# A windowed-attention stage with its exponentials two units ahead, its softmax division on VectorE, and its PSUM banks shared out anew

## The chip, the cores and the metric

The kernel runs on one core of a Trainium2 chip. The metric is device time in microseconds (us) for one launch; lower is better. The profile names the engines PE (TensorE; PEld is its weight load), ACT (ScalarE), DVE (VectorE), POOL (GpSimd) and SP (SyncE, which here issues DMAs).

## The reference

The program is two transformer blocks over `x` of shape (8, 512, 128), f32: windowed attention, a mixture of experts, dense attention, and an FP4 feed-forward layer. The change touches the first attention only. For each of the 8 sequences:

```python
h = layernorm(x) * (1 + ca) + sa
xn = rms_norm(h)
q, k, v = split(xn @ w_qkv.T)            # 16 heads of 64
q, k = rope(q), rope(k)
attn = softmax(where(0 <= q_pos - k_pos <= 32, q @ k.T / 8, -1e9))
x = x + ga * ((attn @ v) @ w_out.T)      # per head, then the output projection
```

## The kernel before, in words

`phase_attention0` writes each engine's program out by hand, in a block per engine. The engines meet only at semaphores, and each takes its own instructions in order. A sequence is cut into four **quads** of four heads, and a quad into four **units** (`t` = 0 to 3) of 128 queries, so a sequence has `UNITS` = 16 units; unit 16 of a sequence is unit 0 of the next. `turns` runs `body(b, last)` once for the first sequence, in a loop for the middle six and once more for the last.

A unit `u` goes through these steps:

- PE `score` (L438, L446) makes masked scores for four heads in `psS`, two banks for each parity of `u`, two units ahead of the unit whose turn it is.
- DVE `maxes` (L621) takes the row maxima of the whole unit, also two ahead.
- ACT `exps` (L549) makes the exponentials with their sums: four instructions of 96 columns, each followed by a read of its accumulator. It is called in halves of two heads, `j` = 0 and 1, one unit ahead.
- DVE `inverse` (L653) inverts two sums, and POOL `divide` (L732) multiplies the two heads' `prob` by them, per half.
- PE transposes `prob` into `psT` (L504), ACT copies it to `probT` (L601), PE multiplies by `v` into `psO` (L524), and ACT `copy_oT` (L583) copies the product one unit later.

Beside the units, the projections of the quad after next are made in six **pieces** (`PIECES`), placed by `PLAN`. In each quad four pieces are halves of q and k (L459) and two are v (L464), which `VALUE` numbers. All go through one bank, `psQ`, which ACT `piece` copies out (L560, L565). A q or k piece then has three followers: SP `swap` (L765) sends four DMAs that exchange rotary halves, POOL `cosines` (L722) multiplies the piece by the cosine table, and, two units later, DVE `sines` (L627) multiplies the swapped copy by the sine table and `rope` (L636) adds the two. DVE runs `sines` and `rope` in the midst of its other work for the unit. `windows` (L770 to L772) copies v with DMAs into the layout that L524 reads.

At the end of a sequence `out_project` (L480, 64 instructions) goes through `psQ` too, after a wait for all pieces. DVE then multiplies and adds the result to `x` (L710, L712) and measures it (L365) before it goes on to the next unit's work. `turn_x` (L474), after unit 7's product, brings in the next sequence's input and also waits for all pieces made so far.

This is what ACT does in one unit, and what PE does around the product:

```python
exps(b, u + 1, 0)                        # ACT
wait(act, turned, b * UNITS + u + 1)
nc.scalar.copy(probT[:, :, :], psT[0:KW, :, :]).then_inc(probT_ready, 1)
exps(b, u + 1, 1)
copy_oT(b, u - 1)
for q, m in pieces_at(g, t, last):
    piece(b, q, m)
```

Of the kernel before, what the change touches and what calls it, by code (L numbers as in the profile page):

```python
# [367 lines left out]
def phase_attention0(nc, k):  # L368
# [5 lines left out]
    with ExitStack() as ctx:  # L374
# [15 lines left out]
        psO = ctx.enter_context(nc.psum_tensor("psO", [P, 2, 512], F32))  # L390
        psQ = ctx.enter_context(nc.psum_tensor("psQ", [P, 512], F32))
# [16 lines left out]
        VALUE = (2, 5)  # L408
        PLAN = ((0,), (1, 2), (3,), (4, 5))

        def half_of(m):
            return m - m // 3
# [17 lines left out]
        def _(pe):  # L430
# [21 lines left out]
            def project(b, q, m):  # L452

                wait(pe, piece_out, b * QUADS * PIECES + q * PIECES + m)
                g = q % QUADS
                if m not in VALUE:
                    half = half_of(m)
                    col = (half % 2) * H0 * D + (2 * g + half // 2) * P
                    last = nc.tensor.matmul(psQ[:, :], k.wqkvT[:, col:col + P], xnT[:, :], start=True, stop=True)  # L459
                else:  # L460
                    col = 2 * H0 * D + g * 4 * D
                    for i in range(2):
                        t = 2 * VALUE.index(m) + i
                        last = nc.tensor.matmul(psQ[:, i * 4 * D:(i + 1) * 4 * D], xnT[:, t * P:(t + 1) * P],  # L464
                                                k.wqkvT[:, col:col + 4 * D], start=(i == 0), stop=True, skip_group_check=True)
                last.then_inc(projected, 1)

            def turn_x(b, pieces):
# [4 lines left out]
                for t in range(TILES):  # L473
                    last = nc.tensor.transpose(psQ[:, t * P:(t + 1) * P], xn[:, t, :], k.ident)  # L474
                last.then_inc(x_turned, 1)

            def out_project(b, pairs, first, last_):
                for t in range(TILES):
                    for p in pairs:
                        last = nc.tensor.matmul(psQ[:, t * C:(t + 1) * C], oT[:, p, t * P:(t + 1) * P], k.woT[:, p, :],  # L480
# [14 lines left out]
            def body(b, last):  # L495
                for u in range(UNITS):
# [16 lines left out]
                    for q, m in pieces[:1]:  # L513
# [3 lines left out]
                    wait(pe, oT_ready, b * UNITS + u - 1)  # L517
                    if t == 0:
                        wait(pe, v_placed, (b * QUADS + g + 1) * 48)
                    for i in range(2):  # L520
                        for a in range(2):
                            for j in range(2):
                                hd = slice((2 * i + j) * D, (2 * i + j + 1) * D)
                                ins = nc.tensor.matmul(psO[D * j:D * j + D, u % 2, i * P + a * HALF:i * P + (a + 1) * HALF],  # L524
# [3 lines left out]
                    for q, m in pieces[1:]:  # L528
                        project(b, q, m)
# [13 lines left out]
        def _(act):  # L543
            def exps(b, u, j):
                s = u % 2
                if j == 0:
                    wait(act, max_ready, b * UNITS + u + 1)
                for i in range(2):
                    last = nc.scalar.activation(prob[:, s, 2 * j + i, :], psS[:, s, j, i * KW:(i + 1) * KW], ACT.Exp,  # L549
                                                bias=nmax[:, s, 2 * j + i:2 * j + i + 1],  # L550
# [1430 lines left out]
```

## Time and profile before

| | |
|---|---|
| time, median of 3 runs | 1468.14 us (1468.02 to 1470.77) |
| the profiled execution's own time | 1453.94 us |
| its span | 1452.1 us |
| mean granted TensorE clock | 0.852 |
| busy over the whole span | PE 1064.6, DVE 787.6, POOL 660.8, ACT 615.4 us |
| the stage that changes | about 34 to 700 us of the span |

The profiled execution is 14.2 us below the median of the runs. The units of the changed stage begin near 78 us, after a start in which twelve pieces are projected one after another, and end near 690 us. Its sequences are told apart by L710, which DVE executes once in each.

### The profile page before, as it was taken

To read this page: it belongs to the slowest core of one execution; us is meant where nothing else is said; L and a number is where in the kernel's file an instruction comes from. 1 tells how busy PE (TensorE), PEld (TensorE's weight loads), DVE (VectorE), ACT (ScalarE), POOL (GpSimd) and SP (SyncE) were. 2 spreads that over 40 slices of the span, in tenths; PEclk is the share of its full clock that TensorE was granted. 3 is DMA by queue.
4 is the path that set the end of the run, shared out by engine and by line. 5 is a ranking of instruction groups with operands and counts; after the bars stand their busy time and mean duration, and the time that the engine had idled before them with its cause. 6 is when DMAs were issued, how large, how long until landed. Compare 5 with 4: busy or idle time off the path is not lost. (4 is left out here: it accounts for less than half of the span.)

```text
span 1452.1 us, 26107 instructions
## 1 busy us (share of the span) xinstructions
PE 1064.6 (73%) x8506; PEld 698.1 (48%) x8506; DVE 787.6 (54%) x1755; ACT 615.4 (42%) x2039; POOL 660.8 (46%) x575
## 2 busy tenths in 40 slices
PE   2688888888889888888612596675299999636665
PEld 1245555555556555556502264344056666424444
DVE  4265555656564656543656441112236665488985
ACT  1257464757575666655101231221045555323222
POOL 1366474757575766653100678786200000145451
PEclk9579899999999999999555798888569999868777
DMA  9234243433334342431401144344200000000000
GB/s 258 68 87 110 63 103 88 103 92 99 97 82 112 79 119 73 108 85 37 118 2 55 36 74 69 61 90 78 67 1 1 1 0 0 1 0 7 15 14 22
DMA packets 85374, 93.57 MB, mean 64 GB/s; under 512 B 18752, under 2 KB 58032, under 8 KB 85312
## 3 DMA queue, kind: packets, MB, share of 16 engines
q1 hardware_dynamic: 73184, 81.50, 21.5%
q0 software_dynamic: 11840, 10.76, 5.1%
q8 instruction: 34, 0.56, 0.2%
q10 hardware_dynamic: 288, 0.53, 0.1%
q14 instruction: 28, 0.23, 0.1%
HBM read 24.36 MB, written 10.70 MB: 24 GB/s over the span
## 5 line engine op out<-in xcount | busy, mean ns | idle before, releaser
L732 POOL TENSOR_TENSOR prob<-prob,prob_rsum 128x192 f32<-128x192 f32 x256 | 202.4, 791 | 219.8 <-DVE prob_rsum L653 219.8
L722 POOL TENSOR_TENSOR qk_cos<-qk_raw,const 128x512 f32<-128x512 f32 x128 | 179.4, 1402 | 31.2 <-ACT qk_raw L560 30.5
L549 ACT ACTIVATE prob<-psS,neg_max 128x96 f32<-128x96 f32 x512 | 171.5, 347 | 18.6 <-DVE neg_max L621 18.6
L459 PE MATMUL psQ<-a_xnT,weights 128*128 128x512 f32 x256 | 161.0, 714 | 8.6 <-ACT v_tok L565 4.4
L627 DVE TENSOR_TENSOR qk_swapped<-qk_swapped,const 128x512 f32<-128x512 f32 x128 | 105.1, 821 | 104.7 <-DMA qk_swapped<-qk_raw 103.7
L504 PE MATMUL psT<-const,prob 128*96 128x128 f32 x512 | 95.5, 288 | 59.2 <-POOL prob L732 58.9
L636 DVE TENSOR_TENSOR qk_roped<-qk_cos,qk_swapped 128x512 f32<-128x512 f32 x128 | 124.5, 973 | 2.1
L1308 POOL DMA_INDIRECT ex_rows<-rows,ex_index x64 | 66.4, 1038 | 127.1 <-DMA ex_index<-lists 107.9
L524 PEld LDWEIGHTS psO<-probT,v_windows 96*64 96x64 f32 x2048 | 73.6, 143 | 103.2 <-issue 67.2
L1318 POOL DMA_INDIRECT sums<-ex_y,ex_index x64 | 103.1, 1611 | 29.6 <-issue 18.6
L549 ACT ACTIVATION_READ_ACCUMULATOR prob<-psS,neg_max 128x1 f32 x512 | 107.2, 209 | 0.0
L601 ACT COPY probT<-psT 96x512 f32<-96x512 f32 x128 | 74.3, 580 | 74.8 <-PE psT L504 73.1
L560 ACT COPY qk_raw<-psQ 128x512 f32<-128x512 f32 x128 | 76.4, 597 | 49.8 <-PE psQ L459 44.8
L504 PEld LDWEIGHTS psT<-const,prob 128*96 128x96 f32 x512 | 51.8, 127 | 89.2 <-POOL prob L732 73.7
L1254 ACT ACTIVATE ex_hidden<-ex_psH,ex_b 128x512 f32<-128x512 f32 x64 | 43.5, 687 | 117.2 <-PE ex_psH L1214 61.9
L524 PE MATMUL psO<-probT,v_windows 96*64 96x64 f32 x2048 | 91.6, 235 | 2.1 <-ACT probT L601 2.0
L1214 PE MATMUL ex_psH<-ex_hT,ex_w 128*128 128x512 f32 x128 | 72.8, 714 | 26.0 <-ACT ex_hidden L1254 25.2
L464 PE MATMUL psQ<-weights,a_xnT 128*128 128x256 f32 x256 | 78.3, 432 | 10.5 <-ACT qk_raw L560 5.1
L326 POOL TENSOR_TENSOR rstd<-a_veps,neghalf 128x4 f32<-128x4 f32 (+1 forms) x8 | 8.5, 1057 | 167.9 <-DVE a_veps L320 167.9
L1518 PEld LDWEIGHTS a_psO<-a_v,a_probT 128*128 128x128 f32 x512 | 65.8, 198 | 36.9 <-ACT a_probT L1566 27.6
L621 DVE TENSOR_REDUCE neg_max<-psS 128x4 f32<-128x384 f32 x128 | 70.3, 549 | 23.2 <-PE psS L446 23.2
L653 DVE RECIPROCAL prob_rsum<-prob_sum 128x2 f32<-128x2 f32 x256 | 40.2, 157 | 74.9 <-ACT prob L549 74.7
(282 smaller groups left out, 2120.4 us busy)
## 6 DMA issues: line engine op xcount, KB each, us to landing
qk_swapped<-qk_raw SPq DMA_DIRECT2D x512, 64.0 KB, 2.0
v_windows<-v_tok SPq DMA_DIRECT2D x32, 384.0 KB, 4.4
v_windows<-v_tok SPq DMA_DIRECT2D x32, 256.0 KB, 3.6
mod<-mod_rows SPq DMA_DIRECT2D x8, 512.0 KB, 7.7
ex_w<-in_L_ffn_W SPq DMA_DIRECT2D x16, 256.0 KB, 3.1
v_windows<-v_tok SPq DMA_DIRECT2D x32, 96.0 KB, 2.1
x<-in_L_attn_x POOLq DMA_DIRECT2D x4, 512.0 KB, 12.6
rows<-rt_h SPq DMA_DIRECT2D x8, 256.0 KB, 2.4
```

Of the source, the lines that this page charges most:

```text
L459: last = nc.tensor.matmul(psQ[:, :], k.wqkvT[:, col:col + P], xnT[:, :], start=True, stop=True)
L464: last = nc.tensor.matmul(psQ[:, i * 4 * D:(i + 1) * 4 * D], xnT[:, t * P:(t + 1) * P], k.wqkvT[:, col:col + 4 * D], start=(i == 0), stop= ...
L504: ins = nc.tensor.transpose(psT[0:KW, i, :], prob[:, u % 2, i, :], k.ident)
L524: ins = nc.tensor.matmul(psO[D * j:D * j + D, u % 2, i * P + a * HALF:i * P + (a + 1) * HALF], vw[:, par, a, t, hd], probT[:, 2 * j + i, a ...
L549: last = nc.scalar.activation(prob[:, s, 2 * j + i, :], psS[:, s, j, i * KW:(i + 1) * KW], ACT.Exp, bias=nmax[:, s, 2 * j + i:2 * j + i + ...
L560: ins = nc.scalar.copy(raw[:, half, :], psQ[:, :])
L601: nc.scalar.copy(probT[:, :, :], psT[0:KW, :, :]).then_inc(probT_ready, 1)
L627: nc.vector.tensor_tensor(swp[:, half, :], swp[:, half, :], k.const[:, K_SIN:K_SIN + T], ALU.mult).then_inc(sin_done, 1)
L636: nc.vector.tensor_tensor(qk[:, q % 2, half // 2, half % 2, :], rcos[:, half, :], swp[:, half, :], ALU.add).then_inc(roped, 1)
L722: nc.gpsimd.tensor_tensor(rcos[:, half, :], raw[:, half, :], k.const[:, K_COS:K_COS + T], ALU.mult).then_inc(cos_done, 1)
L732: nc.gpsimd.tensor_tensor(heads, heads, rsum[:, u % 2, 2 * j:2 * j + 2].unsqueeze(2).to_broadcast([P, 2, KW]), ALU.mult).then_inc(normed_r ...
L1318: nc.gpsimd.indirect_dma_start(k.sums, bass.IndirectOffsetOnAxis(ap=index2[:, par, n:n + 1], axis=0), y[:, par, n, :], None, compute_op=AL ...
```

## The change

The code does five things.

- **Exponentials.** `exps` is no longer called in halves. ACT's unit is now: copy `probT`, copy `oT`, all four exponentials of unit `u + 2`, then the pieces.
- **Division.** POOL's `divide` is gone. DVE's `divide` inverts all four sums in one instruction, waits for it, and multiplies all four heads in one instruction of 384 columns. It opens DVE's unit, for unit `u + 1`; `sines`, `maxes` of `u + 2` and `rope` follow.
- **Banks.** `psO` shrinks from two banks to 256 columns of one, and `psQ` grows from one bank to two, used in turn by the parity of the piece. PE's wait before a piece is for the piece before the last one.
- **Plan.** v pieces are now numbers 3 and 5 instead of 2 and 5, and both pieces of a unit with two come before the product.
- **Waits.** The product of unit `u` waits for the copy of unit `u - 1`'s product, where it waited for that of unit `u - 2`.

```diff
-        psO = ctx.enter_context(nc.psum_tensor("psO", [P, 2, 512], F32))
-        psQ = ctx.enter_context(nc.psum_tensor("psQ", [P, 512], F32))
+        psO = ctx.enter_context(nc.psum_tensor("psO", [P, 2 * P], F32))
+        psQ = ctx.enter_context(nc.psum_tensor("psQ", [P, 2, 512], F32))
...
-        VALUE = (2, 5)
-        PLAN = ((0,), (1, 2), (3,), (4, 5))
+        VALUE = (3, 5)
+        PLAN = ((0,), (1,), (2, 3), (4, 5))
...
-                wait(pe, piece_out, b * QUADS * PIECES + q * PIECES + m)
+                wait(pe, piece_out, b * QUADS * PIECES + q * PIECES + m - 1)
...
-                    last = nc.tensor.matmul(psQ[:, :], k.wqkvT[:, col:col + P], xnT[:, :], start=True, stop=True)
+                    last = nc.tensor.matmul(psQ[:, m % 2, :], k.wqkvT[:, col:col + P], xnT[:, :], start=True, stop=True)
...
-                        if i % 2 == 0:
-                            wait(pe, normed_ready, b * 2 * UNITS + 2 * u + i // 2 + 1)
+                        if i == 0:
+                            wait(pe, normed_ready, b * UNITS + u + 1)
...
-                    for q, m in pieces[:1]:
+                    for q, m in pieces:
                         project(b, q, m)
 
                     wait(pe, probT_ready, b * UNITS + u + 1)
-                    wait(pe, oT_ready, b * UNITS + u - 1)
+                    wait(pe, oT_ready, b * UNITS + u)
...
                     ins.then_inc(applied, 1)
-                    for q, m in pieces[1:]:
-                        project(b, q, m)
...
-                    more = not (last and u + 1 >= UNITS)
-                    if more:
-                        exps(b, u + 1, 0)
                     wait(act, turned, b * UNITS + u + 1)
                     nc.scalar.copy(probT[:, :, :], psT[0:KW, :, :]).then_inc(probT_ready, 1)
-                    if more:
-                        exps(b, u + 1, 1)
                     if u > 0:
                         copy_oT(b, u - 1)
+                    if not (last and u + 2 >= UNITS):
+                        exps(b, u + 2)
                     for q, m in pieces_at(g, t, last):
                         piece(b, q, m)
...
-            def inverse(b, u, j):
-
-                wait(dve, exp_done, b * 2 * UNITS + 2 * u + j + 1)
-                nc.vector.reciprocal(rsum[:, u % 2, 2 * j:2 * j + 2], psum_[:, u % 2, 2 * j:2 * j + 2]).then_inc(rsum_ready, 1)
+            def divide(b, u):
+
+                n = b * UNITS + u + 1
+                wait(dve, exp_done, n)
+                nc.vector.reciprocal(rsum[:, u % 2, :], psum_[:, u % 2, :]).then_inc(rsum_ready, 1)
+                wait(dve, rsum_ready, n)
+                nc.vector.tensor_tensor(prob[:, u % 2, :, :], prob[:, u % 2, :, :],
+                                        rsum[:, u % 2, :].unsqueeze(2).to_broadcast([P, 4, KW]), ALU.mult).then_inc(normed_ready, 1)
...
+                    if more:
+                        divide(b, u + 1)
                     if roping:
                         sines(b, q, half)
-                    if more:
-                        inverse(b, u + 1, 0)
+                    if not (last and u + 2 >= UNITS):
+                        maxes(b, u + 2)
                     if roping:
                         rope(b, q, half)
-                    if not (last and u + 2 >= UNITS):
-                        maxes(b, u + 2)
-                    if more:
-                        inverse(b, u + 1, 1)
...
-                    if not (last and u + 1 >= UNITS):
-                        divide(b, u + 1, 0)
-                        divide(b, u + 1, 1)
```

On DVE, one unit in the third quad of a sequence stood like this before (L653 inverts sums, L627 is `sines`, L636 `rope`, L621 `maxes`):

```order
L627 TENSOR_TENSOR qk_swapped<-qk_swapped,const 128x512 [waits swapped2]
L653 RECIPROCAL prob_rsum<-prob_sum 128x2 [waits exp_done]
L636 TENSOR_TENSOR qk_roped<-qk_cos,qk_swapped 128x512 [waits scored,cos_done,sin_done]
L621 TENSOR_REDUCE neg_max<-psS 128x4 [waits scored]
L653 RECIPROCAL prob_rsum<-prob_sum 128x2 [waits exp_done]
```

A unit in the changed kernel (L649 and L651 are the division, L622 `sines`, L616 `maxes`, L631 `rope`):

```order
L649 RECIPROCAL prob_rsum<-prob_sum 128x4 [waits exp_done]
L651 TENSOR_TENSOR prob<-prob,prob_rsum 128x384 [waits rsum_ready]
L622 TENSOR_TENSOR qk_swapped<-qk_swapped,const 128x512 [waits swapped1]
L616 TENSOR_REDUCE neg_max<-psS 128x4 [waits scored]
L631 TENSOR_TENSOR qk_roped<-qk_cos,qk_swapped 128x512 [waits scored,cos_done,sin_done]
```

`maxes` has moved from behind `rope` to ahead of it, and it now stands behind both the wait for the exponentials and the multiplication of 384 columns.

On ACT, a unit with two pieces before, from its first exponential on (L601 copies `probT`, L583 `oT`, L560 and L565 the pieces):

```order
L549 ACTIVATE prob,prob_sum<-psS,neg_max 128x96 [waits max_ready]
L549 ACTIVATE prob,prob_sum<-psS,neg_max 128x96
L601 COPY probT<-psT 96x512 [waits turned]
L549 ACTIVATE prob,prob_sum<-psS,neg_max 128x96 x2
L583 COPY oT<-psO 128x2x128 [waits applied]
L560 COPY qk_raw<-psQ 128x512 [waits roped,projected]
L565 COPY v_tok<-psQ 128x512 [waits projected]
```

The same in the changed kernel (L547 exponentials, L596 `probT`, L581 `oT`, L558 and L563 pieces):

```order
L596 COPY probT<-psT 96x512 [waits turned]
L581 COPY oT<-psO 128x2x128 [waits applied]
L547 ACTIVATE prob,prob_sum<-psS,neg_max 128x96 [waits max_ready]
L547 ACTIVATE prob,prob_sum<-psS,neg_max 128x96 x3
L558 COPY qk_raw<-psQ 128x512 [waits roped,projected]
L563 COPY v_tok<-psQ 128x512 [waits projected]
```

The exponentials are now those of two units ahead, and both piece copies stand right behind the last of them.

## Rows read from the trace of the kernel before

**Rows 1.** Busy time by windows, third sequence: window, PE, PEld, DVE, ACT, POOL, clock, DMA.
```profile
241.00:318.00 77.00, 67.32 (x743) 43.24 (x742) 46.10 (x97) 48.39 (x193) 48.80 (x49) 0.96 0.37 94
```
**Rows 2.** Instructions of line L710, once per sequence: durations in ns, first and last start.
```profile
L710 DVE TENSOR_TENSOR y_mul<-psQ,mod x8: 690/692/693, 162.8 to 687.9; 128x512 f32<-128x512 f32 x8
L710 DVEq FUSED_REGOPS  x6: 82/82/82, 241.1 to 622.5; - x6
```
**Rows 3.** Waits from 85 to 690 us: us in total, times, longest.
```profile
DVE qk_swapped L627 <- DMA qk_swapped<-qk_raw: 88.6, 56, 3.9
...
PE psT L504 <- POOL prob L732: 57.1, 98, 2.1
```
**Rows 4.** Timeline of PE in unstalled units: start, duration, line, what it writes and reads.
```profile
278.28 0.60 PE L504 MATMUL psT<-const,prob 128*96 128x128 f32 x4
...
281.14 0.42 PE L504 MATMUL psT<-const,prob 128*96 128x128 f32 x2
...
285.07 1.13 PE L464 MATMUL psQ<-weights,a_xnT 128*128 128x256 f32 x4
```
**Rows 5.** Timeline of ACT and DVE: exponentials, their followers, and a maximum.
```profile
78.58 0.34 ACT L549 ACTIVATE prob<-psS,neg_max 128x96 f32<-128x96 f32 x1 [1.18 <-DVE neg_max L621]
...
79.76 0.22 ACT L549 ACTIVATION_READ_ACCUMULATOR prob<-psS,neg_max 128x1 f32 x1
...
266.13 0.22 ACT L549 ACTIVATION_READ_ACCUMULATOR prob<-psS,neg_max 128x1 f32 x1
266.38 0.17 DVE L653 RECIPROCAL prob_rsum<-prob_sum 128x2 f32<-128x2 f32 x1 [1.56 <-ACT prob L549]
...
322.33 0.55 DVE L621 TENSOR_REDUCE neg_max<-psS 128x4 f32<-128x384 f32 x1
...
322.92 0.34 ACT L549 ACTIVATE prob<-psS,neg_max 128x96 f32<-128x96 f32 x1 [2.08 <-DVE neg_max L621]
```
**Rows 6.** Timeline of DVE at a sequence's end.
```profile
318.17 0.69 DVE L710 TENSOR_TENSOR y_mul<-psQ,mod 128x512 f32<-128x512 f32 x1 [9.56 <-PE psQ L480]
...
319.01 0.69 DVE L712 TENSOR_TENSOR x<-x,y_mul 128x512 f32 x1 [0.16 <-DVE y_mul L710]
...
320.91 0.69 DVE L627 TENSOR_TENSOR qk_swapped<-qk_swapped,const 128x512 f32<-128x512 f32 x1 [0.18 <-issue]
```
**Rows 7.** Groups of DVE, 241.1 to 318.2 us: count, busy us, mean ns, idle before.
```profile
L347 DVE TENSOR_SCALAR a_h<-x,mean,rstd 128x128 f32 x4 | 1.3, 381 | 0.0
```
**Rows 8.** Timeline of DVE where its instructions meet one of POOL.
```profile
81.81 1.76 DVE L627 TENSOR_TENSOR qk_swapped<-qk_swapped,const 128x512 f32<-128x512 f32 x1
...
83.60 1.64 DVE L636 TENSOR_TENSOR qk_roped<-qk_cos,qk_swapped 128x512 f32<-128x512 f32 x1
```
**Rows 9.** Timeline of POOL over the same stretch.
```profile
82.98 1.71 POOL L722 TENSOR_TENSOR qk_cos<-qk_raw,const 128x512 f32<-128x512 f32 x1
```
**Rows 10.** Timeline: a piece copied by ACT, and the cosine product that follows on POOL.
```profile
300.25 0.58 ACT L560 COPY qk_raw<-psQ 128x512 f32<-128x512 f32 x1 [0.30 <-PE psQ L459]
...
300.92 1.26 POOL L722 TENSOR_TENSOR qk_cos<-qk_raw,const 128x512 f32<-128x512 f32 x1
```
**Rows 11.** Timeline of PE: the output projection.
```profile
310.58 7.41 PE L480 MATMUL psQ<-weights,oT 128*128 128x128 f32 x64 [0.68 <-ACT v_tok L565]
```
**Rows 12.** Timeline of PE at its longest stall of a sequence.
```profile
245.94 0.49 PE L504 MATMUL psT<-const,prob 128*96 128x128 f32 x2 [2.12 <-POOL prob L732]
```
**Rows 13.** Busy time by windows behind that stall, columns as in rows 1.
```profile
246.00:253.00 7.00, 6.36 (x43) 3.64 (x44) 5.03 (x11) 2.83 (x11) 4.80 (x5) 0.51 0.11 28
```
**Rows 14.** Timeline of PE projecting pieces before the first unit.
```profile
47.21 2.07 PE L459 MATMUL psQ<-a_xnT,weights 128*128 128x512 f32 x2 [0.68 <-ACT qk_raw L560]
```
**Rows 15.** Timeline: the four DMAs of one swap, issued by SP.
```profile
320.87 2.42 SPq L765 DMA_DIRECT2D qk_swapped<-qk_raw  x4
```
**Rows 16.** DMA issues by line: count, KB each, median us to landing.
```profile
qk_swapped<-qk_raw SPq DMA_DIRECT2D x512, 64.0 KB, 2.0
v_windows<-v_tok SPq DMA_DIRECT2D x32, 384.0 KB, 4.4
```

More of the change, by code:

```diff
@@ L473, in turn_x @@
                 for t in range(TILES):
-                    last = nc.tensor.transpose(psQ[:, t * P:(t + 1) * P], xn[:, t, :], k.ident)
+                    last = nc.tensor.transpose(psQ[:, 0, t * P:(t + 1) * P], xn[:, t, :], k.ident)
                 last.then_inc(x_turned, 1)
@@ L543, in _, with exps @@
         def _(act):
-            def exps(b, u, j):
+            def exps(b, u):
                 s = u % 2
[L546 to L550, printed above, removed]
-                                                accum_out=psum_[:, s, 2 * j + i:2 * j + i + 1])
+                wait(act, max_ready, b * UNITS + u + 1)
+                for j in range(2):
+                    for i in range(2):
+                        last = nc.scalar.activation(prob[:, s, 2 * j + i, :], psS[:, s, j, i * KW:(i + 1) * KW], ACT.Exp,
+                                                    bias=nmax[:, s, 2 * j + i:2 * j + i + 1],
+                                                    accum_out=psum_[:, s, 2 * j + i:2 * j + i + 1])
                 last.then_inc(exp_done, 1)
@@ L559, in piece @@
                         wait(act, roped, b * HALVES * QUADS + HALVES * (q - 1) + half + 1)
-                    ins = nc.scalar.copy(raw[:, half, :], psQ[:, :])
+                    ins = nc.scalar.copy(raw[:, half, :], psQ[:, m % 2, :])
                 else:
@@ L564, in piece @@
                         wait(act, v_placed, (b * QUADS + q) * 48)
-                    ins = nc.scalar.copy(v[:, first:first + 2, :], psQ[:, :].rearrange("p (t d) -> p t d", t=2))
+                    ins = nc.scalar.copy(v[:, first:first + 2, :], psQ[:, m % 2, :].rearrange("p (t d) -> p t d", t=2))
                 ins.then_inc(piece_out, 1)
@@ L577, in copy_xnT @@
                 wait(act, x_turned, b + 1)
-                nc.scalar.copy(xnT[:, :], psQ[:, :]).then_inc(xnT_ready, 1)
+                nc.scalar.copy(xnT[:, :], psQ[:, 0, :]).then_inc(xnT_ready, 1)
             def copy_oT(b, u):
@@ L583, in copy_oT @@
                 nc.scalar.copy(oT[:, 2 * g:2 * g + 2, t * P:(t + 1) * P],
[L584 removed]
+                               psO[:, :].rearrange("p (i q) -> p i q", i=2)).then_inc(oT_ready, 1)
             squares(0)
@@ L760, in swap @@
             def swap(b, q, half):
-                wait(sp, piece_out, b * QUADS * PIECES + q * PIECES + (1, 2, 4, 5)[half])
+                wait(sp, piece_out, b * QUADS * PIECES + q * PIECES + (1, 2, 3, 5)[half])
                 for n in range(4):
```

27 lines of the change are left out of this document (9 added, 18 removed).

## The prediction

> **What bounds the kernel now.** I read the busy time by windows first. In the third sequence PE is busy 67.3 of 77 us, and no other engine more than 49 [rows 1]. The starts of L710 give the pitch of a sequence: from the first at 162.8 to the seventh at 622.5 is 6 x 76.6 us, and the last takes 65.4 [rows 2]. The waits say what PE lacks: 57.1 us over the stage, 98 times, for POOL's division, while DVE loses 88.6 us to the swap DMAs [rows 3]. An unstalled unit with one piece takes PE 2.86 us (278.28 to 281.14), and a second piece adds about 1.06 (1.13 less its overlap) [rows 4]: 3.4 on average. So PE is near its limit and the rest is waiting for softmax. That looks like an invitation to put softmax further ahead. The question is whether the new order of the softmax engines can keep a pitch of 3.4.
>
> **The new loop.** By the orders shown, DVE multiplies unit u+1, then does `sines`, then `maxes` of u+2. ACT then makes the exponentials of u+2, and DVE's next unit opens by waiting for exactly those. Nothing in this ring can run ahead, although the exponentials are "two units ahead". I count from the end of one multiplication, M, to the next:
>
> - `sines`, 0.69 us [rows 6], and 0.03 to the next instruction: 0.72.
> - the maximum, 0.55, and about 0.02; ACT starts 0.04 after its end (322.88 to 322.92) [rows 5]: together 0.61.
> - four exponentials, from 78.58 to the end of the fourth accumulator read at 79.98: 1.40 [rows 5].
> - the inversion, 0.04 after ACT's end and 0.17 long [rows 5]: 0.21.
> - the wait of DVE for its own result: 0.16, as before L712 [rows 6].
> - the multiplication. Nothing in the trace is this instruction. 384 columns with one input from PSUM take 0.55 [rows 5], 512 with two inputs from SBUF 0.69 [rows 6]. I take 0.56 and keep 0.51 to 0.69.
>
> The sum is 3.66. `rope` runs while ACT is busy, and PE's 3.4 fits beneath.
>
> **The collision.** ACT copies a q or k piece directly behind the exponentials, so it is out about 0.5 us after their end, and POOL begins its cosine product 0.09 later (300.83 to 300.92) [rows 10]. That is 0.57 after the end of the exponentials; the multiplication runs from 0.37 to 0.93. What then happens stands in the trace. POOL's cosine product at 82.98 arrives during DVE's `sines`, which ends at 83.57. It ends 1.12 later, at 84.69, and DVE's next product, which had started at 83.60, ends at 85.24, 0.55 after POOL [rows 8, 9]. Alone they take 1.26 [rows 10] and 0.69. So they take turns, and a waiting POOL goes ahead of the next DVE product. In the new loop this puts the cosine product between the multiplication and `sines`: `sines` ends at M + 1.12 + 0.55 = M + 1.67 instead of M + 0.72. That is 0.95 more on the ring, 4.61 us a unit. It comes in every unit whose predecessor made a piece, at the same place, because ACT's order fixes it. Before, `maxes` and the exponentials had no division ahead of them on DVE.
>
> The Trainium skill (SBUF — State Buffer, "Who interferes with whom") says the same of a DVE instruction with two SBUF inputs against a GpSimd one that reads SBUF: whoever starts first has the shared interface for the whole instruction. It speaks against this change, since a product moves from the one side to the other in front of the instruction that all wait for.
>
> **The sum, middle sequences.** From one L710, the next unit's work starts on DVE 2.74 later (318.17 to 320.91) [rows 6], and inversion, wait and multiplication end at 3.6. The first unit meets no cosine product: 3.66. Then 14 x 4.61 = 64.5, which is 71.8. After the sixteenth multiplication come `sines`, maximum and exponentials, 3.7, and only then the two last pieces, 0.95, for which the output projection waits. Before, it waited 0.68 for a piece [rows 11]; now PE stands idle some 3 us there. It then runs 7.41 us [rows 11], and L710 follows 0.18 later: 84.1. Four layer-norm instructions, 1.3 us [rows 7], come in unit 1 and four similar ones in unit 6; DVE has 0.7 spare in a unit, so they add 1.0 together: 85.1.
>
> Then the clock. After PE's stall of 2.12 us before 245.94 [rows 12], the next 7 us were granted 0.51, the 1.2 GHz level [rows 13]. The new idle stretches of about 3 us, ahead of the output projection and ahead of `turn_x`, which also waits for pieces, should do the same, now with 7.4 us of solid PE work behind. Half speed over 3.4 to 7 us costs 1.7 to 3.4 there, and `turn_x` adds 0 to 1.5. If the clock does not fall it is nothing. I take 2.5, between 0 and 5. The pitch is 87.6 against 76.6: **six times 11.0, 66 us**.
>
> **The first sequence.** Twelve pieces took 2.07 each with 0.68 of waiting for ACT [rows 14], 33 us, from 44.5 on. Two banks remove the 0.68. At the slow clock they then take 24.8, and the first exponentials come at 71.5 rather than 78.6 [rows 5]. If the clock rises, SP is the limit: four swaps of 2.42 [rows 15], then the v windows with 4.4 to landing [rows 16], for which a v piece waits: about 66.5. I take 68.5, a gain of 10. The second multiplication then ends at 74.5. Fifteen units at 4.61, then 3.7 + 0.95 + 0.05 + 7.41 + 0.18, layer norm 1.0 and the clock's 2.5 put L710 at 159.4 instead of 162.8: **3 us less**.
>
> **The last sequence.** No pieces after unit 7: after the first unit's 3.66 come eight units at 4.61, one at 3.66 and four at 2.94 (no `sines`), so the last multiplication ends 59.6 after L710. Transposes, copies and product take 2.4, the projection 7.4, the clock perhaps 1.5: 71 instead of 65.4: **5.5 us more**.
>
> **What costs nothing.** POOL loses about a third of its work, which nothing else waits for. The 88.6 us of DMA waits go: a swap lands about 4 us after its piece (2.42 of issues, 2.0 for the last) [rows 15, 16], and `sines` comes two units, over 7 us, behind. The v piece, now a unit later, no longer meets its windows. The single `psO` bank makes the product wait for a copy that ACT makes directly behind `probT`, under 0.4 us, which PE's scores and projections cover. All of these were waits of engines that now wait for the ring, so their removal pays nothing. What was a projection behind the product is now ahead of it, and PE has over a microsecond a unit to spare.
>
> Together -3 + 66 + 5.5 is **68 us more**. The profiled execution would become 1453.9 + 68 = 1522; I add the same to the median of the runs, 1468.1, which is 14 above it: **1536 us**.
>
> **Rivals.**
>
> - **No collision, so the change pays.** If the cosine product does not get in between (POOL does not overtake `sines`), the ring stays at 3.66. There are 15 + 90 + 8 = 113 collided units, 107 us in all: 1429 us, faster than before. The decision lies at a pitch of about 4.0, that is a loss of 0.35 instead of 0.95. For it speaks that this exact pair of instructions was never seen; against it that rows 8 and 9 show a DVE product started 0.03 behind another and still overtaken. The Trainium skill (GPSIMD Engine Reference, "Key points") holds that VectorE is about twice as fast elementwise, so by that page the move alone is a gain. Chance 0.13.
> - **The multiplication does not shut POOL out.** Then the cosine product starts 0.36 before M and ends at M + 0.90, and `sines` ends at M + 1.45: 0.22 less a unit, 1511 us. With this I count the smaller bounds of the other terms; it lies inside the forecast's own range.
> - **PE becomes the bound through its clock.** At the slow level a unit with two pieces takes PE 7.8 us, more than the ring's 4.61. PE would idle over 1 us in most units. Should the level fall again and again, and not only at the two long gaps, each sequence loses perhaps 5 us more: 1575 us. Against it: PE has some 4 us of slack against the ring, and full work brought the clock back. Chance 0.07.
> - **Gain and loss cancel.** A partial collision, or a start that gains 15 us, could end within 0.2% of before. Chance 0.03.
>
> **How the numbers follow.** The forecast itself has 0.77, with a range of its own from 1500 to 1562 (clock 0 to 5 a sequence, multiplication 0.51 to 0.69, the start by 5 us either way). For a range that holds 8 in 10 I go down toward the faster cases, to 1465, and stop at 1562. About 0.2% (3 us) is what a measurement of this kernel can tell from no change. Slower by more has 0.77 + 0.07 = 0.84, less 0.02 for a larger error in my ring: 0.82. No difference has 0.03. Faster has 0.13 and those 0.02: 0.15.
>
> **What would show it.** In the new profile L622 should average near 1.5 us instead of 0.8, starting next to L651 with POOL's cosine product ending inside it. ACT should wait for `maxes` in each unit, and PE for DVE's `prob`. DVE should no longer wait for the swap DMAs. Before L480 there should be about 3 us of idle PE and a clock near 0.5 in it. The gaps between copies of `probT` should be an even 4.6 us, where they alternated between long and short. The L710 starts should be some 87 us apart and the first near 159. If L622 stays at 0.7, the collision is not there, and the time falls below 1468.

## The result: slower, by less than forecast

The changed kernel takes 1481.51 us (median of 3 runs, 1480.01 to 1483.95) against 1468.14 before, a ratio of 1.0087 (95% interval 1.006 to 1.0115). The forecast was slower, at 1536 us. The direction and the mechanism hold; the size was 68 us forecast against 13 measured. The result lies in the wide range of 1465 to 1562 only because its lower end had been drawn toward the faster rivals, which did not come; the forecast's own range, 1500 to 1562, missed it. In the profiled executions the difference is 27.6 us (spans 1479.7 and 1452.1), because the profiled execution of before lay 14.2 us under its own median and the changed one lay on its median. With many more runs of before, below, the changed kernel stands 23 us above it (1.0163, 1.0137 to 1.0188).

Now the profile after. Over the whole span, DVE rose from 787.6 to 890.0 us and POOL fell from 660.8 to 465.5. The new multiplication is only 128 x 0.56 = 71 of DVE's 102 us more.

```profile
PE 1054.2 (71%) x8506; PEld 717.2 (48%) x8506; DVE 890.0 (60%) x1755; ACT 610.4 (41%) x2039; POOL 465.5 (31%) x319
```

The groups of DVE in one sequence of the changed kernel (316 to 398.4 us; count, busy us, mean ns, idle before) say where it went:

```profile
L622 DVE TENSOR_TENSOR qk_swapped<-qk_swapped,const 128x512 f32<-128x512 f32 x16 | 26.0, 1625 | 0.0
L631 DVE TENSOR_TENSOR qk_roped<-qk_cos,qk_swapped 128x512 f32<-128x512 f32 x16 | 10.8, 676 | 0.0
L651 DVE TENSOR_TENSOR prob<-prob,prob_rsum 128x384 f32<-128x384 f32 x16 | 8.9, 558 | 0.6
L616 DVE TENSOR_REDUCE neg_max<-psS 128x4 f32<-128x384 f32 x16 | 8.7, 546 | 1.4 <-PE psS L446 1.4
L649 DVE RECIPROCAL prob_rsum<-prob_sum 128x4 f32<-128x4 f32 x16 | 2.8, 177 | 10.3 <-ACT prob L547 10.0 <-issue 0.2
```

The new multiplication costs 8.9 us a sequence. But `sines` costs 26.0 for sixteen instructions, which would be 11.0 at the 0.69 that one takes alone. The timeline shows one turn of the ring, from one inversion to the next (426.41 to 430.80, 4.39 us):

```profile
426.25 0.60 ACT L558 COPY qk_raw<-psQ 128x512 f32<-128x512 f32 x1
...
426.41 0.18 DVE L649 RECIPROCAL prob_rsum<-prob_sum 128x4 f32<-128x4 f32 x1 [0.79 <-ACT prob L547]
426.62 0.56 DVE L651 TENSOR_TENSOR prob<-prob,prob_rsum 128x384 f32<-128x384 f32 x1
...
426.93 1.38 POOL L718 TENSOR_TENSOR qk_cos<-qk_raw,const 128x512 f32<-128x512 f32 x1 [0.22 <-ACT qk_raw L558]
427.10 1.76 DVE L622 TENSOR_TENSOR qk_swapped<-qk_swapped,const 128x512 f32<-128x512 f32 x1
...
428.78 0.54 DVE L616 TENSOR_REDUCE neg_max<-psS 128x4 f32<-128x384 f32 x1
...
429.36 0.34 ACT L547 ACTIVATE prob<-psS,neg_max 128x96 f32<-128x96 f32 x1 [1.77 <-DVE neg_max L616]
...
430.80 0.18 DVE L649 RECIPROCAL prob_rsum<-prob_sum 128x4 f32<-128x4 f32 x1
```

POOL's cosine product arrives while the multiplication runs, starts its real work when that ends (427.18) and ends 1.13 later (428.31). `sines`, begun at 427.10, ends 0.55 after that. This is the pattern of [rows 8, 9], now inside the loop that everything waits for. The waits (70 to 720 us: total, times, longest) answer to [rows 3]:

```profile
ACT prob L547 <- DVE neg_max L616: 185.6, 126, 3.8
...
DVE prob_rsum L649 <- ACT prob L547: 84.7, 105, 1.5
...
PE psO L524 <- ACT oT L581: 37.7, 38, 2.1
...
PE psQ L459 <- ACT qk_raw L558: 29.0, 35, 1.2
...
PE psQ L480 <- ACT v_tok L563: 13.8, 7, 2.3
...
DVE qk_swapped L622 <- DMA qk_swapped<-qk_raw: 8.0, 12, 1.3
...
PE psT L504 <- DVE prob L651: 7.5, 8, 1.6
```

PE's waits for `prob`, 57.1 us before, are down to 7.5, and DVE's for the swaps from 88.6 to 8.0. In their place ACT waits 185.6 us for the maxima. PE gained nothing by that: it now waits for the copies that ACT makes around the late exponentials, of the product (37.7 us) and of the pieces. The sequences are told by L706 (durations in ns, first and last start; the second line gives the second to the seventh), as in [rows 2]:

```profile
L706 DVE TENSOR_TENSOR y_mul<-psQ,mod x8: 691/692/694, 152.5 to 713.0; 128x512 f32<-128x512 f32 x8
L706 DVEq FUSED_REGOPS  x6: 82/82/82, 233.2 to 644.2; - x6
```

The first is 10.3 us earlier than before. The six middle pitches are 82.0 us on average, where they were 76.6, and the last is 68.8 against 65.4. The last L706 is 25.1 us later than the last L710 was, so all that lies outside this stage accounts for only 2.5 of the 27.6 us.

### The profile page after: what moved, and what is told of

It is laid out like the page before. It is cut to its first block and busy times, and to the rows that moved or that the text cites. A ratio compares the mean times of both kernels' runs of the same rounds, so it can differ in the third digit from the quotient of the medians.

```text
span 1479.7 us, 25282 instructions
## 1 busy us (share of the span) xinstructions
PE 1054.2 (71%) x8506; PEld 717.2 (48%) x8506; DVE 890.0 (60%) x1755; ACT 610.4 (41%) x2039; POOL 465.5 (31%) x319
## 5 line engine op out<-in xcount | busy, mean ns | idle before, releaser
L547 ACT ACTIVATE prob<-psS,neg_max 128x96 f32<-128x96 f32 x512 | 167.7, 339 | 186.7 <-DVE neg_max L616 186.7
L622 DVE TENSOR_TENSOR qk_swapped<-qk_swapped,const 128x512 f32<-128x512 f32 x128 | 196.1, 1532 | 17.0 <-DMA qk_swapped<-qk_raw 16.7
L459 PE MATMUL psQ<-a_xnT,weights 128*128 128x512 f32 x256 | 156.6, 698 | 32.0 <-ACT qk_raw L558 31.2
L524 PEld LDWEIGHTS psO<-probT,v_windows 96*64 96x64 f32 x2048 | 75.3, 144 | 113.9 <-ACT probT L596 60.1
L524 PE MATMUL psO<-probT,v_windows 96*64 96x64 f32 x2048 | 92.4, 235 | 40.7 <-ACT oT L581 37.7
L596 ACT COPY probT<-psT 96x512 f32<-96x512 f32 x128 | 76.1, 595 | 69.6 <-PE psT L504 69.6
L547 ACT ACTIVATION_READ_ACCUMULATOR prob<-psS,neg_max 128x1 f32 x512 | 104.0, 203 | 0.0
L631 DVE TENSOR_TENSOR qk_roped<-qk_cos,qk_swapped 128x512 f32<-128x512 f32 x128 | 90.7, 709 | 0.2
L504 PE MATMUL psT<-const,prob 128*96 128x128 f32 x512 | 84.0, 288 | 7.5 <-DVE prob L651 7.5
L558 ACT COPY qk_raw<-psQ 128x512 f32<-128x512 f32 x128 | 76.2, 595 | 9.2 <-DVE qk_roped L631 5.3
L480 PE MATMUL psQ<-weights,oT 128*128 128x128 f32 x512 | 68.4, 302 | 13.8 <-ACT v_tok L563 13.8
L616 DVE TENSOR_REDUCE neg_max<-psS 128x4 f32<-128x384 f32 x128 | 70.0, 547 | 13.4 <-PE psS L446 13.3
L1602 DVE TENSOR_REDUCE a_nmax<-a_psS 128x1 f32<-128x512 f32 x64 | 43.8, 686 | 55.3 <-PE a_psS L1458 55.3
L446 PE MATMUL psS<-qk_roped 64*64 64x96 f32 (+1 forms) x2048 | 76.7, 264 | 0.0
L649 DVE RECIPROCAL prob_rsum<-prob_sum 128x4 f32<-128x4 f32 x128 | 22.7, 177 | 86.3 <-ACT prob L547 84.9
L464 PE MATMUL psQ<-weights,a_xnT 128*128 128x256 f32 x256 | 71.0, 403 | 4.7 <-ACT v_tok L563 3.3
```

Source lines behind the costliest of these rows:

```text
L446: last = nc.tensor.matmul(psS[a * HALF:(a + 1) * HALF, s, j, i * KW + WIN - lo:(i + 1) * KW], qk[rows, par, i, 0, q0:q0 + HALF], qk[rows, ...
L459: last = nc.tensor.matmul(psQ[:, m % 2, :], k.wqkvT[:, col:col + P], xnT[:, :], start=True, stop=True)
L504: ins = nc.tensor.transpose(psT[0:KW, i, :], prob[:, u % 2, i, :], k.ident)
L524: ins = nc.tensor.matmul(psO[D * j:D * j + D, i * P + a * HALF:i * P + (a + 1) * HALF], vw[:, par, a, t, hd], probT[:, 2 * j + i, a * HALF ...
L558: ins = nc.scalar.copy(raw[:, half, :], psQ[:, m % 2, :])
L622: nc.vector.tensor_tensor(swp[:, half, :], swp[:, half, :], k.const[:, K_SIN:K_SIN + T], ALU.mult).then_inc(sin_done, 1)
```

## The experiments

All ran in four batches on other occasions than the first comparison, each with its own runs of before. Ratios are to those.

### The pair again

The kernel before, unchanged:

> The kernel before, unchanged, profiled once more. Its one profiled execution was 14.2 us below the median of its runs, while the changed kernel's was at its median, so the profiles differ by 27.6 us and the medians by 13.4. Theory A: the profiled execution of before was a lucky one, and a new profile lies near 1468, with the extra time spread outside the first attention. Theory B: the first attention itself falls into one of two patterns, and a profile at 1468 shows its sequences longer than 76.6 us each.

Measured: 1455.23 us (1449.27 to 1461.63, 10 runs) beside 1455.65 (13 runs) of the same kernel. The profiled execution this time took 1461.63. Its span is 7.7 us longer than in the first profile, and 6.6 of these are in the second sequence: 85 us at a clock of 0.88, where the next one again took 77 at 0.96 (columns as in [rows 1]).

```profile
164.00:249.00 85.00, 72.79 (x743) 46.97 (x742) 45.76 (x98) 48.61 (x193) 48.64 (x49) 0.88 0.34 86
249.00:326.00 77.00, 67.39 (x745) 43.34 (x742) 46.21 (x98) 48.39 (x193) 48.78 (x49) 0.96 0.37 94
```

So neither theory fits as put. In this one profile the extra time is that of a single sequence in which the clock fell, not a second pattern of all of them, and not outside the stage. Whether the other runs spread for the same reason was not looked at. Why the three runs of the first comparison lay at 1468, above all of the later medians (1453 to 1461), stays open.

The changed kernel, unchanged:

> The changed kernel, unchanged, as the reference of the experiments. Expected near 1481.5 us, with L706 82 us apart and one unit in 4.39 us where a cosine product stands between the multiplication and the sines.

Measured: 1478.61 us, ratio 1.0163 (1.0137 to 1.0188); the first ratio was 1.0087 (1.006 to 1.0115). The changed kernel repeats well, before less so. I use 1.0163, which rests on 13 runs of before, for the experiments below.

### Maxima ahead of the sines

```diff
-                    if roping:
-                        sines(b, q, half)
                     if not (last and u + 2 >= UNITS):
                         maxes(b, u + 2)
                     if roping:
+                        sines(b, q, half)
                         rope(b, q, half)
```

> The changed kernel with DVE's maxima ahead of its sines (division, maxima, sines, rope). Theory ring and collision: the cosine product and the sines leave the ring, which is then 0.18 + 0.03 + 0.48 + 0.55 + 0.04 + 1.40 + 0.04 = 2.7 us. DVE's own work with one collision (0.21 + 0.48 + 0.55, sines to 1.7 after the multiplication, rope 0.7) is about 3.2, so PE with 3.4 us a unit becomes the limit: the pitch of a sequence falls from 82 to some 68 to 72 us, and the time by 70 to 105 us, to 1375 to 1410. Rival, PE and its clock (idle gaps before the output projection and the change of banks) are what costs: the time moves by less than 10 us.

Measured: 1397.36 us, 0.9589 (0.9561 to 0.9617), 81 us below the changed kernel and faster than before. The work is the same and the collision still happens, as one unit of this kernel shows:

```profile
364.87 0.56 DVE L651 TENSOR_TENSOR prob<-prob,prob_rsum 128x384 f32<-128x384 f32 x1
...
365.18 1.38 POOL L717 TENSOR_TENSOR qk_cos<-qk_raw,const 128x512 f32<-128x512 f32 x1 [12.70 <-ACT qk_raw L558]
365.35 0.55 DVE L616 TENSOR_REDUCE neg_max<-psS 128x4 f32<-128x384 f32 x1
...
365.81 1.29 DVE L622 TENSOR_TENSOR qk_swapped<-qk_swapped,const 128x512 f32<-128x512 f32 x1
365.93 0.34 ACT L547 ACTIVATE prob<-psS,neg_max 128x96 f32<-128x96 f32 x1
```

The maximum is not held up by POOL (0.55 us in the midst of its product), `sines` is (1.29), and the exponentials start while it waits. The ring is rid of both. The rival, that idle PE and its clock were the cost, falls as the main account; what they do cost is measured further down.

### Half of the cosine product

```diff
-                nc.gpsimd.tensor_tensor(rcos[:, half, :], raw[:, half, :], k.const[:, K_COS:K_COS + T], ALU.mult).then_inc(cos_done, 1)
+                nc.gpsimd.tensor_tensor(rcos[:, half, 0:T // 2], raw[:, half, 0:T // 2], k.const[:, K_COS:K_COS + T // 2], ALU.mult).then_inc(cos_done, 1)
...
+            nc.vector.memset(rcos[:, :, T // 2:T], 0.0)
```

This kernel leaves out the cosine product of the second 256 columns, which stay zero, so its result is incomplete. It serves only to see what the shorter product does to DVE.

> The changed kernel with the cosine product on POOL cut to 256 of 512 columns (the other half of its output is a constant zero, so the rotary result is incomplete); everything that waits for it waits as before. Theory collision: POOL holds the sines up for about 0.55 us instead of 1.12, so L622 averages some 0.95 to 1.0 us, and about 113 collided units lose 0.55 us each: 60 us less than the changed kernel, 1415 to 1430. Rival, the long L622 comes from somewhere else (its own operands, the DMAs): the time stays within 10 us of 1481.

Measured: 1432.67 us, 0.9841 (0.9818 to 0.9865), 46 below the changed kernel. The middle sequences take 75.7 us instead of 82.0. In its trace `sines` has a median of 1215 ns, where the changed kernel has 1758 (min, median, max):

```profile
L622 DVE TENSOR_TENSOR qk_swapped<-qk_swapped,const x128: 682/1215/1262, 52.2 to 641.5; 128x512 f32<-128x512 f32 x128
```

POOL's product now has a median of 837 ns instead of 1378. That halves what `sines` loses over 0.68: 0.53 instead of 1.07. A unit of the ring behind a piece takes 3.84 us instead of 4.38, which is the same 0.54. The time was 3 us above the range I gave. With the shorter ring some `sines` now wait for their swap, as this one in a timeline of the same kernel:

```profile
405.41 0.69 DVE L622 TENSOR_TENSOR qk_swapped<-qk_swapped,const 128x512 f32<-128x512 f32 x1 [0.94 <-DMA qk_swapped<-qk_raw]
```

A DVE instruction untouched by the edit became shorter by what was taken from POOL: the collision is shown.

### Pieces copied ahead of the exponentials

```diff
+                    for q, m in pieces_at(g, t, last):
+                        piece(b, q, m)
                     if not (last and u + 2 >= UNITS):
                         exps(b, u + 2)
-                    for q, m in pieces_at(g, t, last):
-                        piece(b, q, m)
```

> The changed kernel, with ACT copying the pieces ahead of the exponentials in every unit. DVE's order is untouched; only the place of the cosine product moves, from behind the multiplication to beside the exponentials. Theory collision: sines in the ring fall from 1.7 to 0.7 us, the long instruction is now rope, which is not in the ring, and the unit takes 3.4 to 3.6: 1380 to 1405. Rival (the ring is long because DVE holds sines and division ahead of the maxima, whatever POOL does): no shorter than 1440, since the exponentials now also wait behind a piece copy.

Measured: 1413.43 us, 0.9679 (0.9644 to 0.9715). DVE's order is untouched here; only the cosine product now falls on `rope`:

```profile
398.50 1.26 POOL L718 TENSOR_TENSOR qk_cos<-qk_raw,const 128x512 f32<-128x512 f32 x1 [1.63 <-ACT qk_raw L558]
398.61 1.69 DVE L631 TENSOR_TENSOR qk_roped<-qk_cos,qk_swapped 128x512 f32<-128x512 f32 x1
...
400.90 0.68 DVE L622 TENSOR_TENSOR qk_swapped<-qk_swapped,const 128x512 f32<-128x512 f32 x1
401.50 0.55 DVE L616 TENSOR_REDUCE neg_max<-psS 128x4 f32<-128x384 f32 x1
...
402.36 0.58 ACT L558 COPY qk_raw<-psQ 128x512 f32<-128x512 f32 x1 [1.50 <-PE psQ L459]
```

The rival (no shorter than 1440 as long as DVE's order stands) falls. The result is 8 us above my range: ACT now waits 1.50 us for a projection with the exponentials queued behind it.

The same only in the units with what waits for all pieces behind them, with `if u in (7, 15)` around the early copies and `if u not in (7, 15)` around the late ones:

> The changed kernel, with ACT copying the two pieces ahead of the exponentials in units 7 and 15 only. Theory (the piece copies behind the exponentials hold up the output projection and the turn of x, and the idle lowers PE's clock): the 2.3 us of idle before L480 go, L480 takes 7.4 instead of 9.0 us, and a sequence is 3 to 5 us shorter: 20 to 35 us less than the changed kernel, 1443 to 1458. Rival (only the ring counts there too): the exponentials come later by what the projection starts earlier, and the time moves by less than 5 us.

Measured: 1452.99 us, 0.9964 (0.9934 to 0.9994), 29 below the changed kernel by the ratios. In the other units the ring stays as it was (`sines` median 1758 ns, 4.38 us a unit). What goes is the wait ahead of the output projection and the time at the lower clock in it, which the changed kernel shows like this (timeline of PE; then the window's clock, columns as in [rows 1]):

```profile
306.68 0.49 PE L480 MATMUL psQ<-weights,oT 128*128 128x128 f32 x2 [2.27 <-ACT v_tok L563]
```

```profile
306.00:311.00 5.00, 4.32 (x24) 4.32 (x25) 0.00 (x0) 0.90 (x3) 1.27 (x1) 0.66 0.34 83
```

The projection took 9.04 us there, from 306.68 to 315.72, against 7.41 [rows 11]. In the experiment it takes 7.41 in each middle sequence and starts 0.06 us behind the product before it. A middle sequence is 4.6 us shorter (77.3 against 82.0). By the starts of the inversions, about 3.3 of these are between the last inversion and L710. The other 1.3 are at the turn of x, where the unit behind the early copies takes 3.31 us: its cosine product no longer falls into the ring. Early copies in all units are some 40 us faster than in these two alone (1413.43 against 1452.99, same batch), which fits a collision off the ring in the other units, less the new waits; the two were not separated.

### The banks and the plan alone

The kernel before with the change's `psO` and `psQ`, `VALUE`, `PLAN`, the pieces ahead of the product and the waits that go with them; exponentials in halves one unit ahead, POOL's division and DVE's order as before:

```diff
-        psO = ctx.enter_context(nc.psum_tensor("psO", [P, 2, 512], F32))
-        psQ = ctx.enter_context(nc.psum_tensor("psQ", [P, 512], F32))
+        psO = ctx.enter_context(nc.psum_tensor("psO", [P, 2 * P], F32))
+        psQ = ctx.enter_context(nc.psum_tensor("psQ", [P, 2, 512], F32))
...
-        VALUE = (2, 5)
-        PLAN = ((0,), (1, 2), (3,), (4, 5))
+        VALUE = (3, 5)
+        PLAN = ((0,), (1,), (2, 3), (4, 5))
```

> The kernel before with the banks, the plan of the pieces, their place ahead of the product and the product's wait of the changed kernel; exponentials in halves one unit ahead, division on POOL and DVE's order stay as before. Theory: the start gains its 10.6 us here as in the changed kernel, the wait of the v copies for their windows goes, and PE's stalls for POOL's division stay, so 1430 to 1446, 10 to 25 us below before; what the changed kernel loses is then all the new order's. Rival: the single product bank or the pieces ahead of the product cost as much as the start gains; then it is level with before or slower.

Measured: 1416.79 us, 0.9714 (0.9681 to 0.9747), a gain of 42 us, well over the 10 to 25 expected. In the profiles the start gives 11 of it, the rest of the first sequence 6, and the six middle pitches 27 (72.2 against 76.6), while the last sequence is 2 longer. Over the six middle sequences ACT's waits ahead of the v copies fell from 70 us (40.0 for the projection, 30.1 for the DMAs of the windows) to 11.6, and PE's waits for POOL's division, which I had expected to stay, from 43.2 to 32.2. How the 27 us divide among these was not separated. So the change has a good half worth 42 us, and the new order of the softmax costs 65 (1.0163 less 0.9714, of 1456).

### The division back on POOL

```diff
-                wait(dve, rsum_ready, n)
-                nc.vector.tensor_tensor(prob[:, u % 2, :, :], prob[:, u % 2, :, :],
-                                        rsum[:, u % 2, :].unsqueeze(2).to_broadcast([P, 4, KW]), ALU.mult).then_inc(normed_ready, 1)
...
+            def multiply(b, u):
+                wait(pool, rsum_ready, b * UNITS + u + 1)
+                nc.gpsimd.tensor_tensor(prob[:, u % 2, :, :], prob[:, u % 2, :, :],
+                                        rsum[:, u % 2, :].unsqueeze(2).to_broadcast([P, 4, KW]), ALU.mult).then_inc(normed_ready, 1)
...
+            multiply(0, 0)
...
+                    if not (last and u + 1 >= UNITS):
+                        multiply(b, u + 1)
                     if not (last and q >= QUADS):
                         cosines(b, q, half)
```

> The changed kernel with the multiplication back on POOL, for all four heads at once, ahead of the cosine product; DVE keeps the inversion at the front of its unit. Theory (it is the ring exponentials, division, sines, maxima, that sets the pace, with what DVE is shut out for): the multiplication of 384 columns leaves DVE, the sines start directly behind the inversion and ahead of POOL, so the ring is 1.40 + 0.04 + 0.18 + 0.7 + 0.5 + 0.04 = 2.9; but rope then waits for POOL's two products (1.0 and 1.1 us), which makes 3.6 to 4.2 a unit: 1390 to 1440. Rival (VectorE is the better place, as POOL is about half as fast): slower than the changed kernel, over 1481.

Measured: 1410.23 us, 0.9673 (0.9637 to 0.9709). With the multiplication off DVE the sines start directly behind the inversion, ahead of POOL:

```profile
406.85 0.18 DVE L649 RECIPROCAL prob_rsum<-prob_sum 128x4 f32<-128x4 f32 x1 [0.87 <-ACT prob L547]
406.95 0.66 DVE L622 TENSOR_TENSOR qk_swapped<-qk_swapped,const 128x512 f32<-128x512 f32 x1
407.11 1.18 POOL L723 TENSOR_TENSOR prob<-prob,prob_rsum 128x384 f32<-128x384 f32 x1 [2.74 <-DVE prob_rsum L649]
407.53 0.55 DVE L616 TENSOR_REDUCE neg_max<-psS 128x4 f32<-128x384 f32 x1
```

POOL is the slower engine for this multiplication (at least 0.82 us against 0.56 on DVE), and yet the better place for it in this order. The exponentials two units ahead with the division there are level with the banks alone (0.9673 and 0.9714, intervals overlapping).

### Combinations

Maxima first, and pieces first in units 7 and 15:

> Both edits together on the changed kernel: DVE's maxima ahead of its sines, and ACT's pieces ahead of the exponentials in units 7 and 15. Theory (the ring and the two late pieces are separate costs): of the 25 us that the second edit gave alone, 10 to 25 remain, since the gaps before L480 are 1.1 to 2.4 us in the kernel with the maxima first: 1372 to 1388, the fastest of all. Rival (PE is the limit in that kernel and the idle gaps are what it has to spare): within 5 us of 1397.

Measured: 1377.69 us, 0.9484 (0.9456 to 0.9511), one of the two best. Of the 29 us that the second edit brought alone, about 15 (by the ratios) are left, so most of that cost is separate from the ring. PE is busy 92% of the middle sequences (377.4 of 412.2 us). That suggests that PE bounds it now, which no run tested:

```profile
138.80:551.00 412.20, 377.40 (x4443) 255.91 (x4442) 325.00 (x582) 288.31 (x1158) 139.04 (x102) 0.99 0.41 105
```

Maxima first, and pieces first in every unit:

> Maxima first on DVE, and pieces ahead of the exponentials in every unit. Theory: with the maxima out of the collision's way already, the collision's place no longer matters, and what copying the pieces first does to the exponentials (they stand behind a projection that may not be ready) costs a little: 1385 to 1405. Rival (the two edits add up, as each takes its own wait away): under 1375.

Measured: 1409.07 us, 0.97 (0.9672 to 0.9728), slower than maxima first alone and 4 us above the range. The waits of this kernel (143 to 580 us) name the reason I gave, at a greater price; with the maxima first alone, ACT has no such wait between 146 and 571 us:

```profile
ACT qk_raw L558 <- PE psQ L459: 75.9, 87, 3.6
```

Maxima first, and the multiplication on POOL (the two diffs above):

> Maxima first on DVE, and the multiplication on POOL. Theory (division on VectorE is worth something once nothing in the ring stands behind it): POOL's product of 384 columns takes 1.0 against 0.5 us, and the sines are shut out for 2.1 instead of 1.1 us: 1400 to 1420, slower than with the division on VectorE (1397). Rival (where the division stands does not matter once the maxima are first, since PE is the limit): within 5 us of 1397.

Measured: 1383.71 us, 0.9526 (0.9497 to 0.9554). Both expectations fall: it is neither slower nor level but faster than maxima first with the multiplication on VectorE (0.9589, 0.9561 to 0.9617). Between 146 and 571 us, DVE is busy 299 us here against 317 with the multiplication on it, and PE's waits for ACT's copies ahead of L524, L474 and L480 are 12 us against 34. So what DVE is spared counts for more than what `sines` loses by being shut out for longer (1083 ns median). How the two shares divide was not separated.

All three edits:

> The changed kernel with all three: maxima first on DVE, multiplication on POOL, pieces ahead of the exponentials in units 7 and 15. The gaps before L480 were only 0.54 us in the kernel with maxima first and multiplication on POOL, against 1.1 to 2.4 with the multiplication on DVE, where the third edit brought 20 us. Theory (the third edit is worth the gap it removes, there and at the turn of x): 5 to 12 us less than 1383.7, so 1371 to 1379, level with or just below the best so far (1377.7). Rival (PE is at its limit near a pitch of 68): no less than 1381.

Measured: 1383.07 us beside 1460.91 of before, 0.948 (0.9448 to 0.9512). The theory's 1371 to 1379 was missed. In us it is the rival's value, but before was slower in that batch too; by the ratio it is level with 0.9484, and its interval overlaps that of 0.9526 as well. So what the third edit adds to the other two is not shown. The two best versions can't be told apart: they have the maxima first and the early pieces in common, and take 75 us off before.

## Why the prediction was right about the sign and wrong about the size

**The ring and the collision: right.** The forecast gave the order multiplication, cosine product, `sines`, maximum, exponentials as what sets the pace, `sines` at 1.5 us on average (1.53 measured), DVE's waits for the DMAs gone, ACT waiting for the maxima in each unit (126 times), and PE idle ahead of L480 with a clock below full in it. The experiments confirm it from three sides: the collision halved, moved off the ring by DVE's order, and moved off it by ACT's order.

**Some signs did not come.** PE was to wait for DVE's `prob`; it does so only 8 times, for 7.5 us in all. What it waits for is the copy of the product before (37.7 us in 38 waits, the longest 2.1), which I had priced at under 0.4 us and covered. And the gaps between the copies of `probT` are not an even 4.6 us: in the third sequence they run from 3.0 to 6.1, although the ring's units behind it are an even 4.4. None of this changed the ring, which kept its 4.38 us.

**The faster rival** ("no collision") was refused. In the middle sequences no unit came down to the rival's 3.66 us, except the first of each, which meets no cosine product. **"The multiplication does not shut POOL out"** was refused too: POOL's product is held until the multiplication ends (426.62 + 0.56 = 427.18) and then takes 1.13. **PE bound by its clock** did not come as a rule: over whole sequences the granted clock was 0.89 to 0.96, and the ring's units of 4.38 us stayed as they were.

**The term that failed is the length of the ring, 4.61 against 4.39.** It is some 29 us of the error. It was made too long in two places. For "the wait of DVE for its own result" I took 0.16 from L712. L651 starts 0.03 after the inversion's end (426.59 to 426.62). The other part is what follows `sines` and the maximum: DVE's records overlap by 0.08 (L616 begins at 428.78, `sines` ends at 428.86), and the exponentials start 0.58 behind the maximum's start instead of 0.61. Both were in the trace of before. L636 in [rows 8] waits for DVE's own `sines` and starts 0.03 after its end, while the 0.16 that I used is a row of a sequence's end. And L621, at 322.33 in [rows 5], begins 0.09 before the end of this one:

```profile
321.73 0.69 DVE L636 TENSOR_TENSOR qk_roped<-qk_cos,qk_swapped 128x512 f32<-128x512 f32 x1
```

The first unit of each sequence of the changed kernel meets no cosine product and shows the ring without the collision:

```profile
401.12 0.18 DVE L649 RECIPROCAL prob_rsum<-prob_sum 128x4 f32<-128x4 f32 x1
...
401.81 0.69 DVE L622 TENSOR_TENSOR qk_swapped<-qk_swapped,const 128x512 f32<-128x512 f32 x1
...
404.43 0.18 DVE L649 RECIPROCAL prob_rsum<-prob_sum 128x4 f32<-128x4 f32 x1 [0.87 <-ACT prob L547]
```

It is 3.31, not 3.66. The collision costs 1.07, not 0.95, so two errors partly cancelled in the 4.61, and that is luck. What is left is 3.5 us a middle sequence.

**The boundary and the layer norm were too long as well, by 2.1 us a middle sequence.** I took 2.5 for the clock and the turn of x; about 1.6 is there: the projection took 9.0 instead of 7.41 in four of the six, 1.1 on average, and the multiplication behind the turn of x came 0.5 late. The layer-norm instructions, priced at 1.0, fit beside the exponentials at 1.10 us for four, where [rows 7] have 1.3. Together the six middle sequences came to 492 us instead of 526.

**The first sequence** was 7 us shorter than forecast. The start was nearly right (first exponentials at 68.0, forecast 68.5; second multiplication done at 73.5, forecast 74.5). Its fifteen units of the ring took 3.8 less, and its boundary 2.1 less. **The last** was 68.8 against 71: the ring 3.6 less, the end behind it 1.4 more.

These terms are 34 + 7 + 2 = 43 of the 68 us, and leave 25, which with 2.5 outside the stage is the 27.6 between the profiles. The other 14 us are the step "I add the same to the median of the runs": it took the profiled execution of before for as far below the median as the changed one would be. Before scatters between 1448 and 1466 in the later batches, and the three runs of the first comparison lay at 1468 to 1471.

**"Their removal pays nothing"** held in the middle sequences of the changed kernel, where the ring sets the pace, but it hid that two opposite halves had been put together. The banks alone are worth 42 us, which the ring then covered. I had priced the whole and not its parts, so the forecast could not say which half to keep.

## What to carry to other kernels

When a step is moved ahead on one engine, follow the ring it makes with the other engine's in-order queue: here the exponentials ran two units ahead by number, and DVE still had to finish one unit's division and sines before it could release the next. Put what another engine waits for first, and behind it the instructions that a GpSimd product can shut out; here that order alone was worth 81 us. Count a ring from the durations between starts of the same kind of pair, not from one exceptional row: here an error of 0.2 us stood in the sum a hundred times.

## What the runs showed of the hardware that was not expected

- An instruction of DVE that waits for DVE's own last result starts 0.03 us after the end of an inversion of 4 columns (L651 behind L649), but 0.16 after that of L706, a product with one input in PSUM (L708 behind it). One that waits for nothing begins 0.08 before the end of the one ahead. Whether the input or the size decides was not tried.
- The lockout works in the other order too. In the kernel with the maxima first, POOL's product at 372.94 held the multiplication, begun 0.06 later, for 1.62 us instead of 0.56:

```profile
372.94 1.27 POOL L717 TENSOR_TENSOR qk_cos<-qk_raw,const 128x512 f32<-128x512 f32 x1 [3.73 <-ACT qk_raw L558]
373.00 1.62 DVE L651 TENSOR_TENSOR prob<-prob,prob_rsum 128x384 f32<-128x384 f32 x1
```

- It also takes in DVE instructions with a single tensor input in SBUF. Four layer-norm instructions take 1.10 us in the changed kernel, with POOL idle, and 2.06 in the kernel with the maxima first, where a cosine product begins 0.13 us after them:

```profile
407.86 1.10 DVE L347 TENSOR_SCALAR a_h<-x,mean,rstd 128x128 f32 x4
```

```profile
367.75 2.06 DVE L347 TENSOR_SCALAR a_h<-x,mean,rstd 128x128 f32 x4
367.88 1.34 POOL L717 TENSOR_TENSOR qk_cos<-qk_raw,const 128x512 f32<-128x512 f32 x1 [1.33 <-ACT qk_raw L558]
```

The Trainium skill (SBUF — State Buffer, "Who interferes with whom") names `tensor_scalar` among the instructions that can take the shared pair of ports, and the traces agree, with 0.96 us more here. The maximum, which reads PSUM, was never held (0.55 us throughout, at most 559 ns in that kernel), which agrees with the same section on `tensor_reduce`.
